# A two-attention network on one core: the engines' loops written out, and the late slices' normalisation moved from GpSimd to VectorE

## What is computed

```python
x = x + attn_a(layernorm(x))   # 16 heads of 16; scores over 2048 keys, softmax
x = x + ffn(layernorm(x))
x = x + attn_b(layernorm(x))   # on the sequence seen as (b, h, dh, t): again 2048 wide, softmax
x = x + ffn(layernorm(x))

# attn_a
q, k, v = split(x @ w_in.T + b_in)
att = softmax(einsum('blhd,bmhd->blmh', q, k) * scale, axis=2)
opt = einsum('blmh,blhd->blhd', att, v) @ w_out.T + b_out   # v of the query's own row
# attn_b
attn = softmax(einsum('bhdt,bhds->bhts', k, v) * temperature, axis=-1)
out = einsum('bhdt,bhts->bhds', q, attn)
# ffn: square(relu(x @ W_fc.T)) @ W_proj.T, then a count of spikes over 5 steps, / 5
```

## Time and profile before

| | |
|---|---|
| median of 3 runs | 2801.47 us |
| the profiled execution | 2799.21 us, its span 2797.4 us |
| busy | VectorE 2509.2 us (90%), ScalarE 2545.7 (91%), TensorE 2383.7 (85%), GpSimd 1301.6 (47%) |
| instructions in the span | 43801 |
| TensorE's clock, mean | 0.970 of full speed |

### The profile page before, as it was taken

How to read it: one execution, slowest core, us unless ns; L and a number is a source line. 1 busy time by engine, 2 the same in 40 slices (tenths; PEclk the granted TensorE clock), 3 DMA queues, 4 the chain that set the end, 5 groups by cost and what they waited for, 6 DMA issues and landing times. The chain is left out here.

```text
span 2797.4 us, 43801 instructions
## 1 busy us (share of the span) xinstructions
PE 2383.7 (85%) x12438; PEld 1044.3 (37%) x12672; DVE 2509.2 (90%) x2590; ACT 2545.7 (91%) x4753; POOL 1301.6 (47%) x1913
## 2 busy tenths in 40 slices
PE   5688878877877787777788999999999999999997
PEld 2244444433433443343342333333333333333334
DVE  5898888899999999999988999999999989999994
ACT  2899898999999999999988999999999989999994
POOL 1246666655554554555452244444434434443445
PEclk8999999999999999999999999999999999999999
DMA  6521212143311111111111111111111111111110
GB/s 201 126 63 45 75 44 75 38 100 76 70 35 43 37 35 36 42 30 34 50 36 50 34 45 42 34 40 44 42 31 46 42 29 47 42 37 37 44 28 16
DMA packets 190988, 141.32 MB, mean 51 GB/s; under 512 B 92163, under 2 KB 177669, under 8 KB 190726
## 3 DMA queue, kind: packets, MB, share of 16 engines
q1 hardware_dynamic: 190726, 138.28, 18.6%
HBM read 92.04 MB, written 41.94 MB: 48 GB/s over the span
## 5 line engine op out<-in xcount | busy, mean ns | idle before, releaser
L1033 DVE TENSOR_REDUCE nmax<-score 128x1 f32<-128x1024 f32 x1024 | 1198.2, 1216 | 136.9 <-PE score L814 129.1
L1006 DVE TENSOR_REDUCE nmax<-score 128x1 f32<-128x1024 f32 x1024 | 1211.0, 1219 | 81.2 <-PE score L752 70.1
L1214 ACT ACTIVATE big<-score,nmax 128x1024 f32<-128x1024 f32 x1024 | 1138.4, 1120 | 83.1 <-DVE nmax L1006 77.2
L1257 ACT ACTIVATE score<-score,nmax 128x1024 f32<-128x1024 f32 x1024 | 1118.7, 1098 | 58.2 <-DVE nmax L1033 55.6
L814 PE MATMUL score<-big,shared 128*128 128x512 bf16 x1956 | 627.5, 404 | 250.9 <-ACT score L1257 216.2
L752 PE MATMUL score<-shared 128*128 128x512 bf16 x1906 | 576.6, 385 | 77.5 <-ACT big L1214 48.9
L733 PE MATMUL bank_g<-big,qw 128*32 128x512 f32 x4096 | 547.4, 608 | 1.0 <-ACT qcol L1242 1.0
L752 PEld LDWEIGHTS score<-shared 128*128 128x128 bf16 x2048 | 137.8, 97 | 609.8 <-ACT big L1214 568.3
L814 PEld LDWEIGHTS score<-big,shared 128*128 128x128 bf16 x2048 | 137.1, 99 | 541.9 <-ACT score L1257 449.1
L708 PEld LDWEIGHTS bank_f<-norms,w_fc_sb 128*128 128x128 f32 x2048 | 278.4, 191 | 75.6 <-ACT hid L1179 36.9
L708 PE MATMUL bank_f<-norms,w_fc_sb 128*128 128x128 f32 x2048 | 296.9, 278 | 10.7 <-ACT hid L1179 9.7
(11 more groups left out here) (141 smaller groups left out, 1671.8 us busy)
## 6 DMA issues: line engine op xcount, KB each, us to landing
shared<-q_parts SPq DMA_DIRECT2D x256, 64.0 KB, 2.4
shared<-kb_parts SPq DMA_DIRECT2D x256, 64.0 KB, 2.3
shared<-vb_parts SPq DMA_DIRECT2D x256, 64.0 KB, 2.3
big<-k_parts SPq DMA_DIRECT2D x48, 192.0 KB, 5.0
big<-k_parts SPq DMA_DIRECT2D x24, 256.0 KB, 7.5
kb_parts<-pieces SPq DMA_DIRECT2D x96, 64.0 KB, 1.6
vb_parts<-pieces SPq DMA_DIRECT2D x96, 64.0 KB, 1.6
shared<-in_x SPq DMA_DIRECT2D x32, 128.0 KB, 2.4
```

The source lines that it names most:

```text
L1006: v.tensor_reduce(nmax[:, par, c // NCH, c % NCH:c % NCH + 1], score_b(turn, c)[:, :], AX.X, ALU.max, negate=True).then_inc(max_b, 1)
L1033: v.tensor_reduce(nmax[:, par, c // NCH, c % NCH:c % NCH + 1], score_a(turn, c)[:, :], AX.X, ALU.max, negate=True).then_inc(max_a, 1)
L1214: a.activation(expo[:, c // NCH, (c % NCH) * CH:(c % NCH + 1) * CH], score_b(turn, c)[:, :], ACT.Exp, bias=nmax[:, par, c // NCH, c % NCH: ...
L1257: a.activation(s[:, :], s[:, :], ACT.Exp, bias=nmax[:, par, c // NCH, c % NCH:c % NCH + 1], accum_out=esum[:, par, c // NCH, c % NCH:c % N ...
```

## The change

The helpers produce all iterations with constants, on all engines. GpSimd keeps the reciprocal deviation (`slice_rstd`), which moves from the end of its iteration to a place ahead of `square` 0; the normalised rows are made by VectorE (`slice_norm`) at c 25, for the next slice, with statistics at c 14 and 16 in place of 17 and 19. GpSimd's split is cut in two: `first_part` stands ahead of the FFN's `normalise`, `other_parts` at the end of the iteration. The first slice is normalised by VectorE before iteration 0.

```diff
-        def iterations(eng, body, unrolled=2 * ROUND_A):
-            for it in range(unrolled):
-                body(it, it % ROUND_A, it // TPB)
-            with eng.Fori(unrolled, T - 2, ROUND_A) as it:
-                for k in range(ROUND_A):
-                    body(it + k if k else it, k, unrolled // TPB)
-            for it in range(T - 2, T + DRAIN):
-                body(it, it % ROUND_A, BATCH - 1)
-        def iterations_b(eng, body):
-            for it in range(1, 8):
-                body(it, it % ROUND_B)
-            with eng.Fori(8, T, ROUND_B) as it:
-                for k in range(ROUND_B):
-                    body(it + k if k else it, (8 + k) % ROUND_B)
-            for it in range(T, T + LIF_LAG):
-                body(it, it % ROUND_B)
+        def iterations(body):
+            for it in range(T + DRAIN):
+                body(it, it % ROUND_A, min(it, T - 1) // TPB)
+        def iterations_b(body):
+            for it in range(1, T + LIF_LAG):
+                body(it, it % ROUND_B)
...
+            def slice_norm(u):
+                dve.wait_ge(s_rstd, 2 * u + 2)
+                need(dve, s_tr, u)
+                dve.wait_ge(s_aggr, SLS * u + SLS)
+                for s in range(SLS):
+                    last = v.tensor_scalar(s_n[:, s, :], s_x[:, u % 2, s, :], s_mv[:, s, 0:1], s_rs[:, s:s + 1],
+                                           ALU.subtract, ALU.mult)
+                last.then_inc(s_xn, 1)
...
                     if u is not None and u + 1 < NSL:
-                        if c == 17:
+                        if c == 14:
                             slice_stats(u + 1)
-                        if c == 19:
+                        if c == 16:
                             slice_aggr(u + 1)
+                        if c == 25:
+                            slice_norm(u + 1)
...
-            def slice_norm(u):
+            def slice_rstd(u):
                 stand_alone(pool, (s_aggr, SLS * u + SLS))
                 g_.tensor_scalar(s_var, s_mv[:, :, 1], EPS, 0.0, ALU.add, ALU.add).then_inc(s_rstd, 1)
                 pool.wait_ge(s_rstd, 2 * u + 1)
                 g_.tensor_tensor(s_rs, s_var, power[:, 0:SLS], ALU.pow).then_inc(s_rstd, 1)
-                stand_alone(pool, (s_rstd, 2 * u + 2), (s_tr, u))
-                for s in range(SLS):
-                    last = g_.tensor_scalar(s_n[:, s, :], s_x[:, u % 2, s, :], s_mv[:, s, 0:1], s_rs[:, s:s + 1],
-                                            ALU.subtract, ALU.mult)
-                last.then_inc(s_xn, 1)
...
+                if w is not None:
+                    first_part(w)
                 if i1 is not None:
                     normalise(i1, 0, ffn_mv, ffn_step, xn[:, :], xin[:, 1 - par, :], ffn_tr, i1).then_inc(ffn_xn, 1)
-                if w is not None:
-                    step_split(w)
                 if i2 is not None:
                     spikes(i2, i2, par, 4, 5)
...
                 if i3 is not None:
                     split_kv(i3)
+                if u is not None and u + 1 < NSL:
+                    slice_rstd(u + 1)
                 if i1 is not None:
                     square(i1, 0)
...
-                if u is not None and u + 1 < NSL:
-                    slice_norm(u + 1)
+                if w is not None:
+                    other_parts(w)
```

More of the change, by code:

```diff
@@ L533, in phase_a @@
                     store_slice(w, u)
-            for it in range(T + DRAIN):
-                phase_a(it, it % ROUND_A, 0)
+            iterations(phase_a)
             def phase_b(it, turn):
@@ L576, in _ @@
             load_b_q(1, 1)
-            for it in range(1, T + LIF_LAG):
-                phase_b(it, it % ROUND_B)
+            iterations_b(phase_b)
             for r in range(2):
@@ L849, in phase_a @@
                         head_product(0, c)
-            iterations(pe, phase_a, 3 * ROUND_A)
+            iterations(phase_a)
             def phase_b(it, turn):
@@ L876, in phase_b @@
                         head_product(i, c)
-            iterations_b(pe, phase_b)
+            iterations_b(phase_b)
         @block.vector
@@ L956, in _ @@
             slice_aggr(0)
+            slice_norm(0)
             def ffn_stats_of(n, par, done, count):
@@ L1059, in phase_a @@
                     if u is not None and u + 1 < NSL:
-                        if c == 17:
+                        if c == 14:
                             slice_stats(u + 1)
-                        if c == 19:
+                        if c == 16:
                             slice_aggr(u + 1)
-            iterations(dve, phase_a)
+                        if c == 25:
+                            slice_norm(u + 1)
+            iterations(phase_a)
             def phase_b(it, turn):
@@ L1087, in phase_b @@
                     last_neuron(T + n, n % 2, n - (T - 3), out_stored[n % 2], 8 * (n - n % 2))
-            iterations_b(dve, phase_b)
+            iterations_b(phase_b)
         @block.scalar
@@ L1283, in phase_a @@
                         project_b(i3, 1 - par, c)
-            iterations(act, phase_a)
+            iterations(phase_a)
             def phase_b(it, turn):
@@ L1306, in phase_b @@
                             ffn_take(T + i3, 1 - par)
-            iterations_b(act, phase_b)
+            iterations_b(phase_b)
         @block.gpsimd
@@ L1334, in slice_norm, with first_part @@
                 g_.tensor_tensor(s_rs, s_var, power[:, 0:SLS], ALU.pow).then_inc(s_rstd, 1)
-                stand_alone(pool, (s_rstd, 2 * u + 2), (s_tr, u))
-                for s in range(SLS):
-                    last = g_.tensor_scalar(s_n[:, s, :], s_x[:, u % 2, s, :], s_mv[:, s, 0:1], s_rs[:, s:s + 1],
-                                            ALU.subtract, ALU.mult)
-                last.then_inc(s_xn, 1)
-            def step_split(w):
+            def first_part(w):
                 if w < NE - 1:
@@ L1350, in step_split, with other_parts @@
                 g_.tensor_tensor(s_res, s_f, s_parts[:, 0, :, :], ALU.subtract).then_inc(s_split, 1)
+            def other_parts(w):
                 stand_alone(pool, (s_split, 4 * w + 2))
@@ L1354, in step_split @@
                 g_.tensor_tensor(s_parts[:, 2, :, :], s_res, s_parts[:, 1, :, :], ALU.subtract).then_inc(s_split, 1)
-            slice_norm(0)
+            slice_rstd(0)
             def normalise(n, which, got, step, dst, src, free, count):
@@ L1510, in phase_a @@
                     result(i2, i2, par, x2_stored[par], 8 * (i2 - par))
-                if u is not None and u + 1 < NSL:
-                    slice_norm(u + 1)
+                if w is not None:
+                    other_parts(w)
                 if head0(it):
                     half_distance(0, 0, 1)
-            iterations(pool, phase_a)
+            iterations(phase_a)
             def add_attention(i, slot):
@@ L1570, in phase_b @@
                     half_distance(i, par, 1)
-            iterations_b(pool, phase_b)
+            iterations_b(phase_b)
 _NAMES = ["x", "w_in", "b_in_col", "b_in_row", "w_out", "b_out", "wq", "bq_col", "wkv", "bkv_row", "temp", "w_fc", "w_proj"]
```

## The result

The changed kernel takes 2759.63 us (median of 4 runs, 2757.28 to 2761.88) beside 2800.77 us for the kernel before in the same session (4 runs, 2797.80 to 2804.88): a ratio of 0.9856, 95% interval 0.9841 to 0.9872. The forecast was 2761 us. The profiled execution took 2757.28 us with a span of 2755.5, so 41.9 us less span than before; the sum had said 40.

A forecast was written before the change was run, and what follows sets the result against it. VectorE (90% busy) and ScalarE (91%) alternate, with VectorE idle mostly where TensorE's scores are late. Slices -25, branches -10 and register operations -5 us make -40, so a median of 2761 us, range 2751 to 2770.

The forecast's parts named there:

- the two waits that the slices were to lose: Slice iterations: TensorE's transposes waiting for GpSimd's rows, 20.4 us, and `ffn_down` waiting for GpSimd's squares, 9.0 us.
- The signs that I had named: Profile after: slice iterations 3 to 10 at 43 to 43.6 us, new rows at 0.41 us; rows over 0.6 would refute.
- 2 x 0.41 = 0.82 us: Iterations 3 to 9: cost of two added VectorE row operations per slice, at the prelude's 411 ns each.
- the sum's upper bound: Slices: the added rows hide beside ScalarE, which is as busy, giving -31 us.
- the rival that VectorE and GpSimd block each other: Slices: 14 new rows slowed by GpSimd's operations, up to 0.75 us each, 10.5 us, total 2772; chance 0.08.
- The gap shrinks by 0.93 us: Slice iterations: VectorE's gap behind `ffn_down` falls from 1.37 to 0.44 us, as GpSimd's squares come earlier.
- ScalarE as what comes next: Slices after the change: ScalarE, busy 41.67 us, is late next, with TensorE's fp32 bursts at c 3 to 12.
- the 42.6 of the sum: Iteration 10, which has no next slice: ScalarE, busy 41.67 us, holds it at about 42.6 us.
- The rival that something would hold the slices at 45 us: Slices: ScalarE's copies and TensorE's fp32 products keep iterations at 45 us, giving back 13 us, total 2774; chance 0.12.
- The branches: -10 us: Iterations 17, 23 and 52, at branches back: excesses of 2.6, 3.3 and 3.8 us go, together -10 us.
- The register operations: -5 us: Attention b: 40.63 us in the loop against 40.40 written out, 24 iterations at 0.2 us; nothing counted in attention a.
- The slower rival: Slices: VectorE waits at c 25 for GpSimd's `s_rstd`, GpSimd some 12 us late, 2817 us at 8 us each; chance 0.04.

The follow-up runs named there:

- split whole: The changed kernel with GpSimd's split in one piece again, behind the FFN's normalisation: 2765.16 us in one run.
- c 24: The changed kernel with VectorE's slice rows one chunk earlier, at c 24: 2756.12 us, ratio 0.9837; when run again 2760.05 us, ratio 0.9850.
- GpSimd's gap: The changed kernel with the slice rows made by GpSimd between spikes 7 and square 1, where it idled: 2756.00 us, ratio 0.9848.

## Why the prediction was right, and where it was not

**Right in time, and in its main causes.** 2761 us was forecast, 2759.63 came, and the two waits that the slices were to lose are gone. But the slices gave 21.4 us and not 25, and that miss was made good by what the sum didn't have in attention b. The signs that I had named say the same: the iterations take 43.9 us and not 43 to 43.6, and the new rows last over 0.6 us, the first of each pair 1.13.

**What missed in the slices is a term that the sum put at nothing: the statistics moved from c 17 and 19 to c 14 and 16.** Taken one by one, with iteration 3 of the kernel before, 43.49 us, as the start:

| term | forecast | measured | from |
|---|---|---|---|
| the split in two | -0.93 | -1.08 | iteration 10, split whole against changed |
| the rows on VectorE | +0.82 | +0.83 | iterations 3 to 9, changed against c 24 |
| the statistics moved | 0 | up to +0.66 | iterations 3 to 9 at c 24 against 10 |
| iteration 3 to 9 | 43.4 | 43.94 | the terms give 43.90 |

The third is read from iterations that differ in more than the statistics (10 also lacks `slice_rstd` on GpSimd), and no run changes it alone; but ScalarE's 0.58 us wait starts right behind them. Seven times the 0.55 us between 43.94 and 43.4, less 0.15 by which iteration 10 came in under its 42.6, are the 3.6 us by which the slices fell short.

**The price of the rows was luck.** "2 x 0.41 = 0.82 us" met the 0.83, but by another way: the two operations take 1.6 us, and about half of that falls into a wait that VectorE had anyway. Undisturbed, at 0.73 us, they cost nothing, as the sum's upper bound had it. I had weighed the rival that VectorE and GpSimd block each other and put it aside because "it does not run in the fast way in which the other was caught". That argument was wrong: 411 ns alone turned into up to 1131 ns. The row for it was there, the square beside a TENSOR_SCALAR at the kernel's end. The rival said 10.5 us for it, and moving the rows away from the square gives back 5.6 to 5.8 in the slices (350.0 against 344.2 to 344.4). So the rival held in mechanism at half its size.

**"The gap shrinks by 0.93 us"** was about right without the rows (1.08 in iteration 10). Once the rows stand where that gap was, the one split in two is worth 0.65 us per iteration.

**ScalarE as what comes next** held in part. Iteration 10 ends at 42.45 us with ScalarE busy 41.4, as the 42.6 of the sum had it. But the 43.11 us at which c 24 and GpSimd's gap both end is not its limit: 0.58 us of it is a wait of ScalarE for VectorE. The rival that something would hold the slices at 45 us failed.

**The branches: -10 us held, nearly.** Iterations 17, 23 and 52 lost 2.7, 3.4 and 4.1 us, of which 0.5 in iteration 17 goes with the clock. In the changed kernel with all four loops back the same three take 1.9, 3.8 and 3.9 us more than their clean neighbours, 9.6 in all. But of the "1 to 2 us" that stay if the clock's dip merely comes elsewhere, something did stay: the mean granted clock over 11 to 30 is 0.96 before and 0.97 after, what the iterations besides 17 and 23 take beyond 40.04 us went from 5.8 us to 6.6, and so the stretch gave 5.2 and not 6. In the other written-out profiles it takes 807.2 to 810.1 us. Of the two rules of the Trainium skill weighed there, the one on instruction fetch (Runtime: NRT & Kernel Launch, Instruction fetch mechanics) fits the runs in kind: the stall comes with the jump back and goes when nothing jumps. The 108 ns for a compare-and-branch (Advanced Engine Details and Errata, Control Flow Timing) are not the price of a jump back here, which is 2.0 to 4.5 us.

**The register operations: -5 us held, and on one engine.** 24 x (40.58 - 40.37) = 5 us. VectorE's loops alone cost 0.3 us per iteration, TensorE's nothing, and with ScalarE's and GpSimd's it is 0.08 less than without. That attention a has no such tax held too: its clean iterations are 40.04 us before and after.

**Iterations 40 to 63 gave 13.5 us, not 9.** Iteration 52 gave 4.1 and the register operations 4.8 to 5. The rest is what the other iterations take beyond a clean one, 7.7 us in the profile before and 3.1 in the one after. Most of that is the loops' too, a cost that the sum didn't have: iterations 49 to 51 and 61 to 63 account for 4.2 us before and 0.4 after, and the two other profiles in which TensorE jumps back show 4.1 and 4.4, none of the written-out ones over 0.5. What is left, 3.5 and 2.7 us, is mostly single waits for `xin` elsewhere, which differ by more than that between two profiles of the same kernel: in the second one of the changed kernel two wait 1.8 us and the stretch is 5.9 us longer. So the total was met because a cost that I had overlooked in the loops paid for one that I had overlooked in the slices.

**The slower rival** needed GpSimd 12 us late. `s_rstd` was never waited for in the changed kernel, and was there 5.8 us early.

## What to carry to other kernels

Before adding a row operation to a busy engine, look at what the other engine runs at that very spot: a start 0.06 us behind GpSimd's square made 1.6 us of 0.73 here, and one chunk up or down the list avoids it. When a change also moves small work along a list, as the statistics here, give the move a term of its own and look for what covered the work where it stood. A loop's branch back cost 2 to 4.5 us each time on whichever engines had the loop, and register arithmetic between the instructions 0.3 us per iteration on VectorE alone; try the loop on one engine at a time to see whose it is. A gap that a change removes is worth its length only if nothing else is then put into it.

## What the runs showed of the hardware that I had not expected

A TENSOR_SCALAR of 128x256 with both scalars from SBUF took 403 to 415 ns alone, 400 to 556 beside GpSimd's one-input operation and up to 1131 beside its TENSOR_TENSOR of 128x512. GpSimd's square lost nothing (1.04 us), its one-input operation about 0.04 us. Jumping back cost some 2 us or more each time; computing the waits in registers cost VectorE 0.3 us per iteration of attention b and TensorE nothing. TensorE's granted clock fell to its lower level now and then in attention a with and without stalls, and the iterations in which it did are the ones that take 40.6 or 40.8 us instead of 40.04. And gains of 5.6 us in a stretch, the same in every profile, did not show in medians of five runs of 2760 us each.
